# Scaling the tail rows of a message on ACT instead of DVE

## The reference

```python
hyper_head = expmap0(head_emb)
hyper_tail = expmap(tail_emb, hyper_head)
hyper_rel = expmap(rel_emb, hyper_head)
res = project(mobius_add(hyper_tail, hyper_rel))
res = logmap(res, hyper_head) + ricci * 1e-07
res = jax.nn.relu(res)
sums = jnp.zeros((n_entities, res.shape[-1]), res.dtype).at[head].add(res)
```

## Time and profile before

| | |
|---|---|
| median of 3 runs | 24790.95 us (24785.87 to 24802.65) |
| profiled execution, in all | 24791.08 us |
| its span | 24789.1 us |
| busy PE / PE weight loads | 12374.2 / 10197.3 us |
| busy DVE | 9344.9 us |
| busy ACT | 2152.3 us |
| busy POOL | 16770.4 us |
| mean granted PE clock | 0.533 |

### The profile page before, as it was taken

How to read it: one execution, slowest core, us unless ns; L and a number is a source line. 1 busy time by engine, 2 the same in 40 slices (tenths; PEclk the granted TensorE clock), 3 DMA queues, 4 the chain that set the end, 5 groups by cost and what they waited for, 6 DMA issues and landing times. The chain is left out here.

```text
span 24789.1 us, 209513 instructions
## 1 busy us (share of the span) xinstructions
PE 12374.2 (50%) x53533; PEld 10197.3 (41%) x53534; DVE 9344.9 (38%) x15329; ACT 2152.3 (9%) x4257; POOL 16770.4 (68%) x16828
## 2 busy tenths in 40 slices
PE   3222222777866777767774435443434333434343
PEld 1111111566655666556663335333333323333332
DVE  6555443777776777711111111211111121111112
ACT  0000000333322333200010000000000000000000
POOL 4777777777756777667735774577467757774776
PEclk6555555555555555555555555555555555555555
DMA  0000000111121111211111111111211121121112
GB/s 23 2 2 2 2 2 10 31 31 31 31 22 35 31 31 31 31 30 27 27 15 27 28 28 16 25 28 28 18 31 28 28 27 28 28 27 22 28 28 27
DMA packets 726161, 584.85 MB, mean 24 GB/s; under 512 B 438936, under 2 KB 512348, under 8 KB 725842
## 3 DMA queue, kind: packets, MB, share of 16 engines
q0 software_dynamic: 528384, 505.04, 13.2%
q1 hardware_dynamic: 197458, 76.88, 1.3%
HBM read 535.07 MB, written 45.88 MB: 23 GB/s over the span
## 5 line engine op out<-in xcount | busy, mean ns | idle before, releaser
L399 POOL DMA_INDIRECT rows<-table_lin,pay x9984 | 9419.4, 943 | 4775.9 <-issue 3001.7
L1336 DVE TENSOR_TENSOR acc<-acc,pair 128x1024 f32 x832 | 1016.1, 1221 | 10676.7 <-PE pair L604 10532.9
L604 PE MATMUL pair<-rows,onehot 128*128 128x64 f32 x19968 | 4799.1, 425 | 0.0
L604 PEld LDWEIGHTS pair<-rows,onehot 128*128 128x128 f32 x19968 | 4492.5, 332 | 520.2 <-issue 520.2
L592 PE MATMUL pair<-ones_bf,zeros_bf 1*128 1x512 bf16 x1664 | 837.5, 603 | 7545.3 <-issue 7516.0
L399 POOL DMA_INDIRECT rows<-table_hyp,pay x3328 | 3405.5, 1023 | 1316.2 <-issue 1018.2
L592 PEld LDWEIGHTS pair<-ones_bf,zeros_bf 1*128 1x128 bf16 x1664 | 109.8, 100 | 7722.5 <-issue 7722.5
L383 POOL DMA_INDIRECT payload_src<-rows x1600 | 1555.2, 972 | 737.7 <-issue 737.7
L383 POOL DMA_INDIRECT payload_dst<-rows x1600 | 1560.3, 975 | 487.2 <-issue 487.2
L564 PE MATMUL pair<-tab,sel_t 128*128 x6656 | 1421.2, 383 | 389.0 <-ACT rel L757 187.3
L564 PEld LDWEIGHTS pair<-tab,sel_t 128*128 128x128 f32 x6656 | 1270.6, 284 | 643.0 <-issue 638.3
(11 more groups left out here) (298 smaller groups left out, 16211.4 us busy)
## 6 DMA issues: line engine op xcount, KB each, us to landing
rows<-table_lin,pay POOLq DMA_INDIRECT x9984, 2.4
rows<-table_hyp,pay POOLq DMA_INDIRECT x3328
payload_src<-rows POOLq DMA_INDIRECT x1600, 2.1
payload_dst<-rows POOLq DMA_INDIRECT x1600, 2.1
pay<-payload_src SPq DMA_DIRECT2D x208, 64.0 KB, 1.8
pay<-payload_dst SPq DMA_DIRECT2D x208, 64.0 KB, 1.8
table_hyp<-tab SPq DMA_DIRECT2D x2, 4900.0 KB
table_lin<-xs SPq DMA_DIRECT2D x3, 3136.0 KB
```

The source lines that it names most:

```text
L399: pool.indirect_dma_start(out=rows[:, h, t, 0:width], out_offset=None, in_=table[:, :], in_offset=bass.IndirectOffsetOnAxis(ap=pay[:, h, t ...
L604: last = nc.tensor.matmul(sums[:, bass.ds(at, D)], onehot[:, h, t, :], mv, start=False, stop=False, skip_group_check=True)
L1336: V.tensor_tensor(flat_acc[:, at], flat_acc[:, at], ps_half[u], ALU.add)
```

## The change

ACT now multiplies the tail rows by their coefficient: for each half, 16 activations (Copy with a scale), one for each tile, as the scale is a column with one value per partition. The first half stands behind quad 4 of the next group's fetch, the second behind quad 5. Both wait for the coefficients. DVE drops its two multiplications of tail rows, multiplies the head rows in one instruction of full width in place of two halves, waits for each half of ACT, and adds. The tail's coefficient stays in `EO` in SBUF and no longer goes to PSUM, so two additions become one. `answered` counts two more in each group, which moves the numbers that PE waits for.

```diff
-ANSWERS = 6
+ANSWERS = 8
...
-                        await_reg(pe, "pe", S["answered", m], ANSWERS * g + (u + 5))
+                        await_reg(pe, "pe", S["answered", m], ANSWERS * g + (u + 7))
...
                     answer(g, h, 3, SQ, SQ, ACT.Sqrt)
                     answer(g, h, 4, A1, A1, ACT.Ln)
+                    for u in range(2):
+                        next(ahead, None)
+                        await_reg(act, "act", S["coefficients", m], MIXES * g + 1)
+                        for t in range(HG * u, HG * u + HG):
+                            tail = nc.scalar.activation(rows[:, h, t, 0:D], rows[:, h, t, 0:D], ACT.Copy, scale=EO[:, 1, t:t + 1])
+                        tail.then_inc(S["answered", m], 1)
                     for _ in ahead:
                         pass
...
-                TT(EO[:, 3, :], EO[:, 3, :], U2, ADD)
-                TT(ps_mix[:, 1, :], EO[:, 1, :], U2, ADD)
+                TT(EO[:, 1:4:2, :], EO[:, 1:4:2, :], both(U2), ADD)
                 dve.drain().then_inc(S["coefficients", m], 1)
+                TT(hd[:, :, 0:D], hd[:, :, 0:D], over(ps_mix[:, 0, :], D), MUL)
+                level()
                 for u in range(2):
                     th, tr = hd[:, half(u), 0:D], t_[:, half(u), 0:D]
-                    TT(th, th, over(ps_mix[:, 0, half(u)], D), MUL)
-                    TT(tr, tr, over(ps_mix[:, 1, half(u)], D), MUL)
-                    level()
+                    answered(m, g, 5 + u)
                     TT(th, th, tr, ADD)
                     dve.drain().then_inc(S["coefficients", m], 1)
```

## The result

The changed kernel takes 25031.3 us (median of four runs, 25022.5 to 25042.3) against 24788.4 us for the kernel before in the same comparison: 1.0097 of it, 95% interval 1.008 to 1.0115, so 243 us slower. The forecast was 25027. The profiled execution took 25037.1 us, 246 us more than that of before (24791.1). Two of the four later comparisons ran on chips where every kernel, the one before too, took about 32 000 us; their times are only compared within themselves.

What follows compares the result with a forecast made beforehand. The prediction took the PE-ACT hand-over in the next group's fetch to bound the kernel: 234 us from ACT's blocks in 102 groups plus 2 us in the last groups, on 24791, gave 25027 us, range 24880 to 25160.

Steps and rivals of the forecast that it cites:

- What bounds: Hyperbolic passes: the next group's fetch, handed between PE and ACT, ends a period; DVE's tail has over 4 us to spare.
- What goes from DVE: DVE's tail: two half multiplications and one addition go, some 2.5 us less per group, worth nothing behind DVE's 4 us wait.
- The pace: ACT's 16-activation blocks: 0.25 us per activation with a scale column, 4.0 us a block; bounds 0.16 and 0.35 us.
- The hand-over: Fetch, quads 4 to 6: blocks outlast ACT's idle gap, delaying copies by 1.79, 2.29 or 3.34 us per group, 234 us.
- covered as worked out: Work queued behind the new waits: DVE's later additions, POOL's second half of `mix`, relus and loads cost nothing further.
- a sign against it: Start of the next group: the prediction is wrong if something other than the last result copy, L757, releases it.
- Quad 7 and the start of the next group then move by the same amount.: End of the fetch: the delay at quad 6, 1.79 to 3.34 us by kind of group, passes on unchanged.
- The sum: Whole kernel: 234 us for 102 groups plus 2 us for the last groups, 236 us on 24791, so 25027 us.
- That the column costs nothing: Rival on ACT's blocks: free scale column, pace 0.16 us, 2.56 us a block, 33 us slower, 24824 us; chance 0.09.
- that the activations don't overlap: Rival on ACT's blocks: 0.35 us per activation, 5.6 us a block, 564 us slower, 25355 us; chance 0.07.
- the rival for faster: PE's clock: pauses shift the high-clock stretch so every group runs like the 53.88 us one, 24609 us; chance 0.04.
- ACT about 1150 us busier: Sign expected in the changed profile: ACT's busy time grows about 1150 us, with 3328 new activations of near 0.35 us.

Runs made afterwards that it cites:

- one_tile: The changed kernel with one activation per block instead of 16, the other 30 tail tiles unscaled; 24846.2 us, 1.0011 of the kernel before.
- one_quad_earlier_3: Third run of the kernel before with quad 4 of the next fetch moved between ACT's answers 3 and 4; 24809.2 us against 24788.6, 1.0008.
- in_the_gaps: The changed kernel with its 32 activations in three blocks between selector and result copies of quads 5, 6, 7; 25145.9 us, 1.0129 of the kernel before.
- shifted_code: The changed kernel with 24 more DVE counter instructions ahead of the second pass; 32217.2 us (1.0019 of the kernel before) on a slow chip, 25017.3 (1.0093) when repeated.

## Why the prediction was right, and where it was not

**What bounds.** That the fetch of the next group ends a period and DVE's tail has some 4 us to spare is shown: one_tile keeps the shorter tail and takes the blocks away, and is not faster than the kernel before. One part of that spare time was spoken for, though: behind every even group 3 us and more of it are the end of DVE's loop, which the prediction took for idle time. What goes from DVE was sized too small, 2.5 us per group against 3.6 measured (368 us in 102 groups), since the first addition of head and tail rows, 2.40 us on average before, takes 1.25 now; as it was priced at nothing either way, the sum doesn't move.

**The pace.** 0.25 us was taken, 0.239 measured, the bounds 0.16 and 0.35. The 91 ns of the bias column carried over (93 ns). By the 33 us for each 10 ns the difference is worth 36 us.

**The hand-over.** 234 us were summed for the copies up to quad 6, 206.9 measured. With the measured pace the reading gives 234 - 36 = 198, so the mechanism was sized right to some 9 us. In the slow-clock group +1.79 us were worked out from quad 4 to quad 6, which at a pace of 0.239 is 32 x 0.011 = 0.35 less, 1.44; the group shown has +1.48. ACT's wait for the coefficients, the second addition (55.4 us after the start expected, 6076.75 - 6021.00 = 55.75 measured) and POOL's second `mix` stayed covered as worked out; the start is released by L757 in 78 groups of 104, and by nothing the profile can name in 24, which the prediction had named as a sign against it.

**"Quad 7 and the start of the next group then move by the same amount."** This step failed, in both directions. Between quads 6 and 7 the groups gave 33 us back; in that piece the granted clock was 0.65 and 0.60 (first and second pass), where it had been 0.54 and 0.53. And in the second pass the start moved by 36.6 us more than the copy, at the loop's end. The stretch up to the logarithm moved by 3.2 and 31.3 us. In the second pass 35 us came in between the copies of quads 2 and 3, where the granted clock fell from 0.74 to 0.60; so a shift of the high-clock stretch fits, but no run separates it.

**The sum.** 207 - 33 + 34 + 30 = 238 us in the passes, 246 in the profiled execution, 243 in the medians, for 236 forecast. That it came so close is in part chance: a pace 5% too high and a clock gain not counted stand against a loop's end and a clock loss not counted. The two passes show it: 2.3 us per group were forecast for either, and they grew by 1.50 and 3.17.

**The rivals.** That the column costs nothing is ruled out by 338 against 245 ns, that the activations don't overlap by a pace of 0.239. The granted clock did rise, as the rival for faster had it, but by 0.04 and 0.01, to 0.61 and 0.60, and not to the 0.66 of its price; one_quad_earlier_3 has 0.67 and is no faster, since then DVE's tail ends the group. Of the signs, "ACT about 1150 us busier" was off: that adds up 3328 durations, and since neighbours overlap, ACT is 759 us busier (2911.0 us for 2152.3).

## What to carry to other kernels

An engine with low total load may still be one half of a hand-over that sets the time; what it can take for nothing is a block shorter than its gap there, not its idle share. Here 2.0 us per gap cost next to nothing (9 us in 102 groups) and 3.9 us cost all that stuck out and the selector copy queued behind it. And spare time of an engine before the start of its next loop turn is not all spare: look at the waits without a releaser and at which turns have them before counting on it, and at what the other engines run at the moment to which the start would move.

## What the runs showed of the hardware that was not expected

- The end of a loop on DVE takes 3.5 us or 5.5 us from the last work before it to the first after it, with the same instructions, against 0.5 to 0.6 us without it. 24 instructions put ahead of the loop changed 5.5 to 3.5. What DVE does in that time no run shows.
- A copy on DVE that starts during POOL's addition of two operands in SBUF (L413, 2.18 us) ends with it: 0.19 us became up to 1.83, in 52 groups of in_the_gaps. An addition on DVE with both operands in SBUF (L1304) took 2.40 us on average in the 104 groups of the kernel before, where it started during POOL's multiplication (L408) and ended 1.08 to 1.09 us after it; it takes 1.25 in the changed kernel, where all but one start after L408 is over. A multiplication with one operand in PSUM (L1302) took 1.21 us beside L413 as well as away from it.
- On two of the chips every kernel took about 1.3 times as long. DVE stands there in nearly every group for up to 5 us at the same few lines, with no releaser. From the list of DVE's waits in shifted_code, on such a chip:

```profile
DVE sc L1216 <- issue: 408.0, 100, 5.1
DVE sc L1212 <- issue: 328.4, 100, 4.4
```

- What is fastest hangs on that: one line more on ACT gave 1% on those chips and nothing on the others.
